# A two-layer transformer kernel: who issues the maximum rows of layer 0's self-attention, and when the late weights are asked for

## The reference, cut to what matters

```python
x_norm = modulate(_ln(x), shift_a, scale_a)
qkv = x_norm @ W_qkv + b_qkv
attn_w = jax.nn.softmax(jnp.einsum('bhqd,bhkd->bhqk', q, k) * scale, axis=-1)
attn_out = jnp.einsum('bhqk,bhkd->bhqd', attn_w, v)
x = x + gate_a[:, None] * (attn_out @ W_proj + b_proj)
...    # layer 0: cross-attention to 77 context tokens, then a gelu MLP, each added to x
...    # layer 1: windowed self-attention, top-16 cross-attention, swiglu MLP, each gated by a vector
```

## Time and profile before

| | |
|---|---|
| median of 3 runs | 471.3 us |
| the profiled execution, first to last instruction | 470.6 us |
| PE busy | 372.1 us (79%) |
| DVE busy | 303.3 us (64%) |
| ACT busy | 204.3 us (43%) |
| POOL busy | 109.5 us (23%) |
| chain that ended last: PE, DVE, ACT, issue | 53%, 28%, 7%, 7% |
| bytes moved by DMA | 12.16 MB, of them some 10.9 MB in the first six of the 40 slices (70.6 us) |

### The profile page before, as it was taken

One profiled execution on the slowest core, in us unless ns is written; L12 is line 12 of the kernel. 1 busy time (PEld: TensorE's weight loads), 2 busy tenths in 40 slices (PEclk: granted clock), 3 DMA queues, 4 the chain that ended last, 5 costly groups with the idle time before them and its releaser, 6 DMA issues.

```text
span 470.6 us, 8977 instructions
## 1 busy us (share of the span) xinstructions
PE 372.1 (79%) x3326; PEld 219.7 (47%) x3326; DVE 303.3 (64%) x1279; ACT 204.3 (43%) x304; POOL 109.5 (23%) x128
## 2 busy tenths in 40 slices
PE   0958839999989988899888788988584566675886
PEld 0735212332333156677655457764362344454454
DVE  4377928999988056666327352234979999996332
ACT  1141016666756935566432133322452555554411
POOL 8047235000010021001014100011434544444010
PEclk9979658999999998999989595556657777776989
DMA  7237560000000000000000000000000000000000
GB/s 212 50 109 219 171 168 1 2 2 3 2 1 2 0 1 1 1 2 3 0 1 1 6 1 7 3 3 0 2 2 1 1 2 1 1 1 1 1 23 24
DMA packets 10811, 12.16 MB, mean 26 GB/s; under 512 B 2378, under 2 KB 9103, under 8 KB 10767
## 3 DMA queue, kind: packets, MB, share of 16 engines
q1 hardware_dynamic: 10469, 11.55, 8.7%
q0 software_dynamic: 256, 0.01, 0.0%
q10 hardware_dynamic: 42, 0.01, 0.0%
HBM read 8.69 MB, written 2.62 MB: 24 GB/s over the span
## 4 chain that ended last, share of the span: by engine, by line
PE 53%; DVE 28%; ACT 7%; issue 7%; DMA 3%; POOL 1%; SPq 1%; ACTq 0%; DVEq 0%
PE psum L1328 6%; PE psum L1388 5%; PE psum L1356 5%; PE psum L1341 5%; DVE mx L1103 4%; DVE left L1158 4%; DVE left L1165 3%; PE psum L1229 3%; PE psum L1487 3%; PE psum L1371 3%; DVE top L1155 3%; PE psum L1399 2%; DVE top L1162 2%; PE psum L1455 2%; PE psum L1411 2%
## 5 line engine op out<-in xcount | busy, mean ns | idle before, releaser
L1103 DVE TENSOR_REDUCE mx<-psum 128x1 f32<-128x512 f32 x128 | 80.1, 681 | 15.1 <-PE psum L1328 15.0
L717 ACT ACTIVATE big<-psum 128x1024 f32<-128x1024 f32 x64 | 62.3, 1022 | 46.0 <-PE psum L1341 45.7
L547 POOL TENSOR_TENSOR rstd<-vareps,minus_half 128x4 f32<-128x4 f32 x12 | 12.2, 1019 | 199.4 <-DVE vareps L887 199.3
L1328 PE MATMUL psum<-KS,QS 72*128 72x512 bf16 x128 | 49.2, 417 | 5.2 <-DVE mx L1103 4.0
L1388 PE MATMUL psum<-kblk,qf 128*128 128x308 f32 x128 | 48.0, 508 | 1.1 <-DVE qf L1036 0.8
L1399 PE MATMUL psum<-ident,pr 128*77 128x128 f32 x256 | 39.6, 306 | 8.9 <-POOL pr L658 8.8
L1341 PE MATMUL psum<-QS,KS 75*128 75x512 bf16 x128 | 39.4, 395 | 7.8 <-issue 7.3
L1399 PEld LDWEIGHTS psum<-ident,pr 128*77 128x77 f32 x256 | 35.7, 172 | 17.2 <-POOL pr L658 12.0
L658 POOL TENSOR_TENSOR pr<-pr,early 128x616 f32<-128x616 f32 x16 | 23.9, 1493 | 56.7 <-ACT early L827 39.5
L1356 PE MATMUL psum<-big,V 128*9 128x512 f32 x256 | 34.3, 608 | 0.5 <-ACT big L717 0.5
L1328 PEld LDWEIGHTS psum<-KS,QS 72*128 72x128 bf16 x128 | 11.7, 102 | 45.7 <-DVE mx L1103 23.7
(11 more groups left out here) (191 smaller groups left out, 677.8 us busy)
## 6 DMA issues: line engine op xcount, KB each, us to landing
QS<-scr_q SPq DMA_DIRECT2D x8, 288.0 KB
KS<-scr_k SPq DMA_DIRECT2D x8, 288.0 KB
scr_q<-qp SPq DMA_DIRECT2D x2, 384.0 KB, 5.6
scr_k<-kp SPq DMA_DIRECT2D x2, 384.0 KB, 6.2
early<-in_L_xcond_w_ada_dram SPq DMA_DIRECT2D x1, 576.0 KB, 8.6
wmlp<-in_L_xcond_W_mlp_dram SPq DMA_DIRECT2D x2, 256.0 KB, 3.4
scr_k<-kp SPq DMA_DIRECT2D x2, 256.0 KB, 6.5
wm<-in_L_xcond_w_m_dram SPq DMA_DIRECT2D x1, 512.0 KB, 7.1
```

The lines of the kernel that those rows point to most:

```text
L717: freed(act.activation(pT[:, u % 2, 1024 * half:1024 * (half + 1)], ps, ACT.Exp), "sT", 0, u, half)
L1103: freed(dve.tensor_reduce(mx[:, n % 3, NT * hh + q:NT * hh + q + 1], ps, AX_X, ALU.max), "max", t, q)
L1328: filled(pe.matmul(ps, QS[b][0:ROWS, h, q * P:(q + 1) * P], KS[b][0:ROWS, h, :], start=True, stop=True), "max", j, q)
```

## The change

`max_rows` of all 8 groups leaves SP's list and goes into POOL's. SP issues the five late weights right behind the stacks. In POOL's list the rows of group 0 stand ahead of `gate_outputs()`, those of group 1 behind it, those of groups 2 to 5 behind `add_bias(0, b)`, and those of groups 6 and 7 behind `ln_rstd(1, 0)` and `add_bias(1, 0)`. The DMAs themselves, their sources, their targets and the semaphores are the same.

```diff
@@ SyncE
-            for n, (b, g) in enumerate(groups):
-                max_rows(sp, b, G * g, G, n, n % 2, s_mrow[n % 2], 3 * (n + 1))
-                if n == 0:
-                    for name, key in (("wso", "w_so"), ("wqc1", "w_q"), ("wco", "w_co"), ("wm1", "w_m1"),
-                                      ("wm2", "w_m2")):
-                        load_w(sp, name, "L1_xcond_" + key)
+            for name, key in (("wso", "w_so"), ("wqc1", "w_q"), ("wco", "w_co"), ("wm1", "w_m1"), ("wm2", "w_m2")):
+                load_w(sp, name, "L1_xcond_" + key)
@@ GpSimd
             spread_qk()
+
+            def rows_of(n):
+                b, g = groups[n]
+                max_rows(pool, b, G * g, G, n, n % 2, s_mrow[n % 2], 3 * (n + 1))
+
+            rows_of(0)
             gate_outputs()
+            rows_of(1)
             for b in range(B):
                 add_bias(0, b)
+            for n in range(2, 6):
+                rows_of(n)
             for n in (1, 2):
                 for b in range(B):
                     ln_rstd(n, b)
                     add_bias(n, b)
+                    if n == 1 and b == 0:
+                        rows_of(6)
+                        rows_of(7)
```

## The result

| | kernel before | changed kernel |
|---|---|---|
| median of 20 runs | 471.5 us (468.55 to 474.88) | 468.22 us (460.92 to 472.64) |
| profiled execution, span | 470.6 us | 463.9 us |

The ratio given for the two is 0.984, with a 95% interval of 0.981 to 0.987; it sets only those runs against each other that are within 1.5% of their kernel's quickest, and the medians of all 20 runs are nearer, 3.3 us or 0.7% apart (468.22 / 471.5 = 0.993). The forecast was 471.0 us with a range from 468.8: the change is faster, by more than I gave it. A second series of both kernels gave a ratio of 0.998 (0.994 to 1.002) and medians 3.5 us apart, so the size of the gain is less sure than the first interval says. In what follows I go by places in the traces and by medians, since single runs of one and the same kernel differ by 6 to 12 us in this table.

The account below looks back on a forecast made before the run. PE's 7.33 us wait for group 0's rows was taken as the hole to attack. Turn 11 -2.8, clock +2.3 and group 6 +0.2 gave -0.3 against the 470.6 span; with the median 0.7 above, 471.0 us, range 468.8 to 473.0.

Parts of the forecast that it names:

- What bounds: Layer 0, 40 to 85 us: PE holds most of the chain, with one large hole of 7.33 us before turn 7.
- the hole at 58.74: PE stands still 7.33 us before turn 7's transposed scores, waiting for group 0's rows; to be gone or under 4 us.
- Rows of group 0: Issued by POOL before the gating, landing at 57.6 or at latest 62.4; either way turn 11's time doesn't depend on it.
- Rows of group 1: Behind POOL's gating, which waits for wso: landing at 77.5, turn 11 gains 2.8 us (bounds 1.7 and 5.3).
- the clock term: PE's clock falls to half in a second hole of 4.5 us before turn 11, costing 2.3 us (0 to 3.5).
- my own sum: -2.8 (turn 11) + 2.3 (clock) + 0.2 (group 6) = -0.3 us against the span of 470.6.
- Turns 7 to 11: PE's time from turn 7's start to turn 11, taken as 14.27 us as before, so turn 11 comes at 73.0.
- Groups 2 to 7: Later rows on POOL: groups 2 to 5 and 7 cost nothing, group 6 a wait of 0.2 us (0 to 1.0).
- (a): The clock doesn't fall in the second hole, or rises at once: 468.7 to 469.7, say 469.2 us; chance 0.25.
- (b): POOL's queue lands late, paid in groups 1 and 6; a loss from 2.7 us landing, 472.6 at 3.3; chance 0.22.
- (c): wso lands much earlier, by 61.4, so the whole 7.33 us is saved: 464 us; chance 0.05.
- (d): DVE slows POOL's DMA issuing, 1.5 us later in groups 1 and 6: +2.7, 474.0 us; chance 0.08.

Follow-up runs that it names:

- SP alone with the rows first: Kernel before, no POOL queue: SP issues group 0's rows between the two batch elements' stacks, late weights behind the stacks, then other groups; median 464.78 us, ratio 0.995.
- the hold alone: Changed kernel, but SP waits until group 0's rows have landed before reading back batch element 1's stacks; median 473.17 us, ratio 0.999.
- group 1 early as well: Changed kernel with batch element 1's stacks held until group 0's rows landed, and group 1's rows issued ahead of POOL's wait for wso; median 465.10 us, ratio 0.982.
- the weights first: Kernel before, but SP issues the late weights ahead of group 0's rows, all rows staying with SP; median 474.56 us, ratio 1.005.

## Why the prediction was wrong, point by point

**What bounds.** Right: the hole at 58.74 was the wait for group 0's rows, and it shrank when they came sooner.

**Rows of group 0.** POOL's first weight is gated at 43.60, and the row at 43.35 still belongs to the spreading; nothing hangs on the 0.25 us. I gave two ends, landing at 57.6 and at 62.4, and said that nothing hangs on which. Measured: 61.3. The end at 62.4 was the near one. Of the some 4.6 us won on the landing (65.9 to 61.3), 3.3 come from the third DMA's earlier issue (57.9 to 54.6) and the other 1.3 or 1.4 from its shorter landing (8.1 to 6.7). Whether those are the other queue or the smaller backlog, no run tells apart.

**Rows of group 1.** wso's landing moved by 0.0, not 0.3; the gating took 8.02 us, as booked; the landing took 1.6 us where I took 2.5. The rows were there at 76.85, forecast 77.5. The gain at turn 11 was 3.4, forecast 2.8: inside the bounds.

**The failing step: the clock.** The gain at turn 11 was the same for both landings of group 0, and so I stopped asking. But the hole in front of turn 11 wasn't: 4.5 us with the one, 0.8 (77.5 less 76.7) with the other. I carried the 4.5 into the clock term and booked 2.3 us for a fall. Measured: a hole of 0.36 us, the granted clock at 1.00 from 71.25 on past 170, loss 0 (changed kernel; us, PE busy, granted clock, DMA share, GB/s):

```profile
71.00:72.00 1.00, 1.00 (x5) 0.93 0.00 0
76.00:77.00 1.00, 0.64 (x3) 1.00 0.03 4
```

The price of a fall was right in the two traces that have a large hole, 2.3 us; the condition for it wasn't met. Whether a hole of 4.5 us would have met it stays open: no kernel had one. With 0 in place of 2.3 my own sum gives -2.6 us, against -3.3 by the medians.

**Turns 7 to 11** took 15.5 us, not 14.27, since the clock rose 9.9 us after turn 7's start (8.4 before). Over the kernels without a large hole ahead of turn 11 it is 14.3 to 17.1 us. With 14.27 the hole would have been 1.2 us (61.34 + 14.27 against 76.85), so that it is as small as 0.36 is in part luck. I took the time as fixed; this is one source of the changed kernel's spread, the landing of group 0's rows the other.

**Groups 2 to 7.** No wait, as forecast for 2 to 5. For group 6 I booked 0.2 us; its DMAs landed in 1.5 to 1.6 us and PE didn't wait at turn 31.

**The rivals.** (a) came in its result, a clock that doesn't fall, with a chance of 0.25; its 469.2 us missed by 1.0. Its reason was another: it kept the hole of 4.5 us and had the clock outlast it. (b) fell: the landing was 1.6 us where it needed 2.7. (c) fell, wso didn't move. (d) fell: POOL's issues took 484 to 604 ns beside DVE's work; where the two did meet, in SP alone with the rows first, it was DVE that was slowed. The price of the Trainium skill, "DMA: Bandwidth & Descriptors", section "Anatomy of one DMA", some 2.0 us for a small POOL DMA, is nearer to the 1.5 to 1.6 on idle engines than my 2.5, and far from the 4.1 to 9.1 under the stacks. In its section "Queues, rings and completion order" the same page has the engines take turns between queues; a queue of its own didn't spare the rows the wait here, with 6.7 to 9.1 us for POOL's slowest and 7.7 for ACT's against 8.1 for q1's.

## What to carry to other kernels

When an argument says that a result is the same at both ends of an unknown, ask it again for each later term: here the time of turn 11 was the same and the hole ahead of it, on which I had hung the clock term, wasn't. For a small urgent transfer beside bulk traffic, a queue of its own brought an earlier issue here (3.3 us) and little in the landing. Holding the bulk back until it had landed brought it down to 1.5 to 1.7 us, but this paid only when the next wait in line was taken away too: 4.6 and then 28.4 us at turns 7 and 11 with the hold alone, 4.6 and 19.4 with group 1 early as well. And before a difference between two traces is explained, take two of one kernel: the same instructions gave spans 4.1 us apart.

## What the runs showed of the hardware that I had not expected

DMAs of 4 KB on a queue of their own, POOL's or ACT's, took up to 7.7 (ACT) and 9.1 us (POOL) from issue to landing while another queue's stacks kept the DMA share at 0.63 to 0.99, and 1.5 to 1.6 us (POOL) with engines next to empty, where SP's took 1.6 to 1.7. An issue held POOL for 0.48 to 0.60 us, where SP took 0.59 at the median. DVE's last part of the split, with two inputs in SBUF, took 1.26 us beside POOL's `add_bias` and 0.28 otherwise. The granted clock came back 8.4 to 14.4 us after PE took up work in turn 7 (66.07 to 74.5 before, 68.04 to 82.4 with the weights first), though the windows show PE busy nearly all that time (4.00 of 4.00 us from 70 to 74 in the kernel before); why it is so long there and 5.7 us after the hole of 8.99, the runs leave open. Nor does a fall need a hole: in the kernel before the clock fell at 53.9, and since it had risen at 50.5 PE had no gap over 0.8 us.
